# Which routed blocks have their rows turned by the DMA engines: every third instead of every fourth

## The reference

```python
# x: (4096, 512); 16 experts, the top 4 of them for each token
topk_idx, w, _ = _route(xf, router_w, correction_bias)
combine = zeros((S, E)).at[arange(S)[:, None], topk_idx].add(w)
g = einsum('sc,ech->esh', xf, gate_w)      # 512 -> 128 for each expert
u = einsum('sc,ech->esh', xf, up_w)
hw = silu(g) * u * combine.T[:, :, None]
routed = einsum('esh,ehc->sc', hw, down_w) # 128 -> 512
shared_out = silu(xf @ shared_gate_w.T) * (xf @ shared_up_w.T) @ shared_down_w.T
x = x + shared_out + routed
```

## Time and profile before

| what | us |
|---|---|
| three timed runs, median | 1027.05 |
| lowest and highest of them | 1024.96 and 1027.68 |
| the profiled execution, time | 1020.97 |
| the profiled execution, span of the core | 1019.2 |
| PE busy in that span | 995.8 |
| DVE busy | 647.9 |
| POOL busy | 442.3 |
| ACT busy | 381.5 |

### The profile page before, as it was taken

One profiled execution on the slowest core, in us unless ns is written; L12 is line 12 of the kernel. 1 busy time (PEld: TensorE's weight loads), 2 busy tenths in 40 slices (PEclk: granted clock), 3 DMA queues, 4 the chain that ended last, 5 costly groups with the idle time before them and its releaser, 6 DMA issues.

```text
span 1019.2 us, 21258 instructions
## 1 busy us (share of the span) xinstructions
PE 995.8 (98%) x6882; PEld 611.1 (60%) x6882; DVE 647.9 (64%) x1526; ACT 381.5 (37%) x776; POOL 442.3 (43%) x508
## 2 busy tenths in 40 slices
PE   8999998999999999999999999999999999999997
PEld 6685653544544444445778778787777854444443
DVE  5956776566178678977545555555555536687767
ACT  3635534433354334331444444444444431111111
POOL 0814601211134322215444454454454337777774
PEclk9979999999999999999999999999999999999999
DMA  9644786558735351412889989899888758999786
GB/s 339 213 163 135 261 272 187 177 154 262 194 111 168 135 145 63 138 49 72 241 262 252 278 264 272 254 256 260 244 249 255 222 172 233 325 301 319 240 256 206
DMA packets 176636, 219.04 MB, mean 215 GB/s; under 512 B 101224, under 2 KB 112360, under 8 KB 175528
## 3 DMA queue, kind: packets, MB, share of 16 engines
q1 hardware_dynamic: 152792, 139.05, 46.3%
q0 software_dynamic: 23760, 78.79, 25.5%
HBM read 124.72 MB, written 70.27 MB: 191 GB/s over the span
## 4 chain that ended last, share of the span: by engine, by line
PE 76%; POOL 9%; DVE 5%; issue 4%; DMA 3%; ACT 1%; SPq 0%; DVEq 0%; POOLq 0%
PE bank L920 19%; PE bank L1046 18%; POOL arena L2028 9%; PE bank L1070 9%; PE bank L936 9%; PE bank L1029 5%; PE bank L1107 3%; PE bank L693 2%; PE bank L715 2%; PE bank L1060 2%; PE bank L1119 2%; PE bank L782 1%; DMA arena<-in_x 1%; DMA arena<-pt_dram 1%; PE bank L703 1%
## 5 line engine op out<-in xcount | busy, mean ns | idle before, releaser
L920 PE MATMUL bank<-arena 128*128 128x512 f16 x960 | 219.5, 380 | 0.8 <-DMA arena<-pt_dram 0.8
L1046 PE MATMUL bank<-arena 128*128 x1716 | 211.0, 273 | 1.2 <-DVE arena L1587 1.0
L1046 PEld LDWEIGHTS bank<-arena 128*128 128x128 f16 x1716 | 163.1, 98 | 26.8 <-issue 2.0
L1983 POOL DMA_INDIRECT arena<-xr_dram,arena x143 | 140.5, 983 | 59.2 <-issue 48.0
L2028 POOL DMA_INDIRECT arena<-y_dram,arena x128 | 139.7, 1092 | 57.1 <-issue 35.4
L920 PEld LDWEIGHTS bank<-arena 128*128 128x128 f16 x960 | 93.7, 99 | 108.9 <-issue 2.2
L1107 PE MATMUL bank<-arena 128*128 128x512 f16 x576 | 128.1, 379 | 0.0
L1308 ACT ACTIVATE arena<-arena 128x512 f16<-128x512 f32 x64 | 40.3, 629 | 223.4 <-DVE arena L1880 111.9
L1070 PE MATMUL bank<-arena 128*128 x429 | 115.4, 378 | 0.0
L1820 DVE SCALAR_TENSOR_TENSOR arena<-bank,arena 128x128 f32<-128x128 f32 x143 | 41.7, 292 | 108.9 <-ACT arena L1360 108.9
L1872 DVE SCALAR_TENSOR_TENSOR arena<-arena 128x512 f32<-128x512 f32 x128 | 96.1, 752 | 23.1 <-DMA arena<-y_dram,arena 19.6
(11 more groups left out here) (221 smaller groups left out, 1308.0 us busy)
## 6 DMA issues: line engine op xcount, KB each, us to landing
y_dram<-arena SPq DMA_DIRECT2D x143, 256.0 KB
arena<-in_x SPq DMA_DIRECT2D x8, 1024.0 KB, 13.5
xr_dram<-arena SPq DMA_DIRECT2D x16, 512.0 KB, 3.2
x_dram<-arena SPq DMA_DIRECT2D x8, 1024.0 KB, 5.7
arena<-in_gu_w SPq DMA_DIRECT2D x16, 512.0 KB, 3.6
out<-arena SPq DMA_DIRECT2D x32, 256.0 KB, 3.9
arena<-x_dram SPq DMA_DIRECT2D x5, 1024.0 KB, 5.4
arena<-x1s_dram SPq DMA_DIRECT2D x20, 256.0 KB, 4.9
```

What stands on the lines that cost most here:

```text
L920: last = mm(bank[half][:, :], (gu_hi_s, gu_lo_s)[wp][:, c, at:at + H], xt[:, xv * KC + kc, :], start=(n == 0), stop=(n == 3 * KC - 1))
L1046: last = mm(bank[2 + j][:, 0:2 * H], rows[:, xv * KC + kc, :], only((gu_hi_r, gu_lo_r)[wp], e, slice(kc * 2 * H, (kc + 1) * 2 * H)), start ...
L1983: pool.indirect_dma_start(out=dst, out_offset=None, in_=xr_dram[:, :], in_offset=bass.IndirectOffsetOnAxis(ap=token_now[:, r:r + 1], axis= ...
```

## The change

Every third block (s % 3 == 2) is turned by the transposing DMA instead of every fourth (s % 4 == 3): 47 blocks instead of 35, so that PE turns 96 blocks instead of 108. The hardware loops of ACT, DVE and POOL hold 12 blocks instead of 8. The blocks that PE turns have four places for gathered rows instead of three, and the fourth place takes the memory of the fourth `y_sb`, so three result buffers are left. The fourth place may be filled for the first time only after the shared expert's fifth block.

```diff
-UNROLLED = 8
+UNROLLED = 12
...
-        xg = view(o2, [4, 2 * D], F16)
+        xg = [view(v, [2 * D], F16) for v in (o2, o2 + 2 * KB, o2 + 4 * KB, o1 + 2 * KB)]
...
-        y_sb = [view(v, [D]) for v in (o1, o3 + 4 * KB, o3 + 6 * KB, o1 + 2 * KB)]
+        y_sb = [view(v, [D]) for v in (o1, o3 + 4 * KB, o3 + 6 * KB)]
...
         def on_tensor(s):
-            return 3 * (s // 4) + s % 4
+            return 2 * (s // 3) + s % 3
...
                 sp.wait_ge(s_xd[h], 16 * (g // 2 + 1))
                 if g >= 2:
-                    sp.wait_ge(s_rg, 4 * g - 4)
+                    sp.wait_ge(s_rg, 3 * g - 3)
                 sp.dma_start_transpose(xdT[h], xd[h]).then_inc(s_dt[h], 16)
...
             for s in range(BLOCKS):
-                y_out(s, s % 4)
-                if s % 4 == 3 and s + 8 < BLOCKS:
-                    turn_fourth(s // 4 + 2, s // 4 % 2)
+                y_out(s, s % 3)
+                if s % 3 == 2 and s + 6 < BLOCKS:
+                    turn_third(s // 3 + 2, s // 3 % 2)
...
-                if s + 2 < BLOCKS and (s + 2) % 4 != 3:
+                if s + 2 < BLOCKS and (s + 2) % 3 != 2:
                     turn_rows(s + 2)
...
-                    act.wait_ge(s_yw[n % 4], 16 * before)
-                A(y_sb[n % 4], bank[6 + n % 2][:, :], ACT.Copy, scale=1.0 / WS).then_inc(s_ye, 1)
+                    act.wait_ge(s_yw[n % 3], 16 * before)
+                A(y_sb[n % 3], bank[6 + n % 2][:, :], ACT.Copy, scale=1.0 / WS).then_inc(s_ye, 1)
...
-            IN_EIGHT = (3, 0, 1, 2, 7, 4, 5, 6)
-            order = [s for g in range(0, BLOCKS, 4) for s in (g + 3, g, g + 1, g + 2) if s < BLOCKS]
+            IN_TURN = (2, 0, 1, 5, 3, 4, 8, 6, 7, 11, 9, 10)
+            order = [s for g in range(0, BLOCKS, 3) for s in (g + 2, g, g + 1) if s < BLOCKS]
...
-                    if s == 7:
+                    if s == 5:
                         pool.wait_ge(s_sd, FIRST * SH)
-                    if s > 7:
-                        pool.wait_ge(s_dt[s // 4 % 2], 16 * (s // 8))
+                    if s > 5:
+                        pool.wait_ge(s_dt[s // 3 % 2], 16 * (s // 6))
                 else:
-                    dst, done = xg[:, s % 4, :], s_xg[s % 4]
-                    if s >= 4:
-                        pool.wait_ge(s_tx, on_tensor(s) - 2)
+                    p = on_tensor(s)
+                    dst, done = xg[p % 4], s_xg[p % 4]
+                    if p == 3:
+                        pool.wait_ge(s_sd, FIRST * SH)
+                    if p >= 4:
+                        pool.wait_ge(s_tx, p - 3)
```

74 lines of the change are left out of this document (37 added, 37 removed).

## The result

| what | before | after |
|---|---|---|
| median of four runs each, us | 1026.01 | 1053.31 |
| lowest and highest, us | 1016.77 and 1027.68 | 1042.13 and 1073.35 |
| profiled execution, time / span, us | 1020.97 / 1019.2 | 1073.35 / 1071.5 |
| PE busy in the span, us | 995.8 | 1015.1 |

The account below looks back on a forecast made before the run. PE was taken to bound the kernel: 5.4 us less turning, less 1.8 us lost at the start, gives 3.6 us less, 1023.5 us against the median of 1027.05; all other terms nothing. Range 1021.3 to 1029.5 us.

Parts of the forecast that it names:

- What bounds the kernel: Routed stage: PE is busy 50.00 of every 50 us, so each us of work taken from PE is worth a us.
- PE's turning: Routed stage: PE turns 12 blocks fewer at 0.45 us each, 5.4 us less; a group of three takes 7.11 us.
- The start: Start of routed stage: block 3's rows are gathered later, PE waits, and 1.8 us are lost (bounds 0.8 to 2.4).
- The deadline of the transposing DMA: PE needs its result 6.2 us after issue; landing taken as 4.8 to 5.5 us, so no wait.
- POOL's order: The xd gather waits for a landing, three gathers follow in a burst; rows still have 1.7 us and more to spare.
- the second rival: Transposing DMA's deadline missed all the time, possibly feeding itself: 1037 us at 6.5 us landing, 1104 at 8.0; chance 0.18.
- the stretch with nine transposing DMAs: Kernel before, 650 to 700 us: nine transposing DMAs with PE still busy 50.00 us, cited against the second rival.
- Room on the DMA engines: Transposing DMAs rise from 5.2 to 7.0 in 50 us; the rate is no bound, only the latency may be.
- Three result buffers: A y write has 6.5 us to land and took 4.0 us in this stage; cost nothing.
- the free start: Start of routed stage costing nothing; the range's low end, given as 1021.3 us; chance 0.10.
- the third rival: Block 3's rows come as early as PE asks, the start costs nothing, gain up to 5.4 us: 1021.7; chance 0.10.

Follow-up runs that it names:

- e11_both_again: The kernel of e5_both run once more, on a fourth chip: 1059.93 against 1060.74 us for the kernel before, ratio 1.001 (0.9964 to 1.0055).
- e3_no_deadline: Changed kernel, every third block's gate_up reading another block's turned rows without waiting for the transposing DMA, which still runs: 1055.15 us, ratio 1.0331 to the kernel before.
- e1_order: Changed kernel with POOL's gathers in the blocks' own order, the xd gather behind its group's other two: 1041.15 us against 1019.7 for the kernel before.
- e10_third_xd: Changed kernel with a third xd place, three places for PE's rows, POOL's loop over 18 blocks: 1078.33 us against 1057.75 for the kernel before, ratio 1.025.
- e9_more_load: Kernel before plus 12 more same-size transposing DMAs, from DRAM, results unused, its own timing kept: 1027.3 us, ratio 1.0012 (0.9964 to 1.0061).
- e6_late_fourth: Kernel before, its 35 transposing DMAs issued two blocks later, some 6 us ahead of use instead of 11: 1055.36 us, ratio 1.0312.
- e5_both: Changed kernel with gathers in the blocks' own order and each transposing DMA issued two blocks earlier: 1020.0 us, ratio 0.996 to the kernel before.
- e4_parts: Kernel before (35 transposing DMAs) with four gather places, three result buffers, ACT's loop of 12 blocks and POOL's of 16: 1026.39 us, ratio 1.0067.

## Why the prediction was wrong

**What bounds the kernel** was read rightly: PE, and only PE, until the change.

**PE's turning** was right. 768 transposes, and a group of 7.10 us where nothing waits, in e11_both_again (forecast 7.11). The 5.4 us were really taken off PE.

**The start** had its mechanism right and its size wrong. PE's timeline of the changed kernel, and the granted clock from 493.7 to 497 us, in answer to the earlier trace rows:

```profile
493.73 1.03 PE L1029 MATMUL bank<-arena 128*128 128x128 f16 x8 [1.85 <-DMA arena<-xr_dram,arena]
494.56 2.70 PE L1046 MATMUL bank<-arena 128*128 x12
497.10 0.28 PE L1060 MATMUL bank<-arena 128*128 128x128 f16 x2
```

```profile
493.70:497.00 3.30, 3.27 (x20) 2.59 (x21) 0.69 (x1) 0.00 (x0) 2.04 (x5) 0.50 1.02 271
```

The wait of 1.85 us stands where it was forecast, but the clock then fell to 0.50, the lower of its two levels (1.2 GHz), for the next 3.3 us. `turn_h` behind that `gate_up` starts 497.10 - 488.52 = 8.58 us into the stage, against 5.25 us before. 3.3 us are lost instead of 1.8.

**The deadline of the transposing DMA** was mis-sized. The 6.2 us were right, the landing wasn't: 4.8 to 5.5 us were taken, 5.7 us was the median, and the tail reached 10.3 us (the row of line 618 over the routed stage):

```profile
DMA to landing us min/median/max: 3.1/5.7/10.3
```

and that of the gathers, line 1982, in answer to the earlier trace rows:

```profile
DMA to landing us min/median/max: 3.5/5.4/9.6
```

A median below the deadline is not "no wait", since nothing gives back what each late one costs. The evidence for 4.8 us came from a few DMAs under a lighter load; all eight of line 628, from 4.6 to 8.0 us with a median of 7.1 us, some of them in the denser stretch behind the routed stage, were set aside for being elsewhere.

**POOL's order is the step that failed.** It said that with 4.8 us to landing the gathers of the burst would be in time, "1.7 us and more are to spare", and that the burst would lengthen the next transposing DMA by "0.3 to 0.7 us, which the 6.2 us hold". By the same working with the medians measured, 5.7 us for the transposing DMA, 2.0 us to the second gather of the burst and 5.4 us for its landing make 13.1 us against the 12.9 us at which PE wants it: the margin is gone before any of the slow ones. e3_no_deadline shows that this path alone can cost the whole loss. e1_order and e10_third_xd, without it, are still at 1.021 (by the medians) and 1.025, so the mis-sized deadline is not the lesser fault: both failed by the same term, a landing of 4.8 us and little more. The feedback was named in the second rival, "it could feed itself", and then dismissed by the stretch with nine transposing DMAs. That stretch had the load but not the timing: nobody waited for a landing there. e9_more_load and e6_late_fourth say the same with the two swapped: load without the timing 1.0012, timing without the load 1.0312.

**Room on the DMA engines** held as far as the rate goes: e5_both moves up to 272 GB/s at a DMA share of 1.00 to 1.12 with PE busy for 48.42 to 50.00 us of 50 in its six stretches. But it was argued as though rate and latency were apart; the median landing rose from 4.2 us in e4_parts to 6.6 us in e5_both.

**Three result buffers** cost nothing in the changed kernel (0.6 us of ACT's waits), nor in e4_parts, where ACT has no such wait. Where PE keeps its pace under the heavier load they may cost: ACT waits for 16.2 us in e5_both, and some of that reaches PE. In the six stretches of e5_both PE stood idle for 2.7 of 300 us. The 5.4 us less work did not shorten its stage (343.6 against 343.7 us); where the rest of them went, I haven't placed.

**The rivals.** The second happened, but not by its own sum: it priced only the wait ahead of `gate_up`, 0.3 us in each of 45 groups, and that wait was 9.6 us by PE's rows. The larger part stands under the gathers, which came last more often. The Trainium skill ("VectorE: DVE Perf Modes", The three transpose paths), which spoke for it, gives 1309 ns for one square by DMA, by estimate 10.5 us for eight. That is no median of this kernel, but the slowest landing here, 10.3 us, comes near it; no run shows why. In the range, the end for the free start should read 1021.7 us, as in the third rival, and not 1021.3; nothing hangs on it.

What stays open: how much of the loss each of the two ways (rows late, turned block late) carries in a usual run, since they trade places between e1, e3 and e6 and can be late together, as at 544.30; the 0.1 to 1.2% of e4_parts; and what three places do. That the cause is the timing (how late the DMA is issued, and what waits for its landing) and not the number of transposing DMAs is shown by e5_both and e6_late_fourth. That a burst lengthens a landing rests on single cases as those of 525.10, 535.29 and 519.13 and on the medians, not on a run in which the burst alone was changed, and beside each of these DMAs writes of y were on their way too; e5_both and e10_third_xd have long landings with hardly a wait of POOL. So the loop as such is not shown.

## What to carry to other kernels

When a kernel gives one engine's work to a DMA, count the lead time of that DMA in the new rhythm and hold it against the tail of landings under the new load, not against a median under the old. Then ask what the landing releases: an issuing engine that starts to wait for a landing sends its next transfers in bursts, and everything that stands behind the wait in its order is late with it. Whether the bursts also lengthen the next landing, so that the lateness feeds itself, was not shown. Issuing earlier together with taking the other gathers out from behind the wait took back all of the loss here.

## What the runs showed of the hardware that I had not expected

- A stall of PE costs more than its length. After idle times of 1.85 and 3.06 us the granted clock stood at 0.50 from 493.7 to 497 us and at 0.63 from 544.3 to 548.9 us, a `gate_up` took 2.70 and 2.66 us instead of 1.47, and it was back at 0.99 and 1.00 in the stretches after that. After a stall of 1.02 us (524.93) the next `gate_up` took 1.52 us, at a clock of 1.00. Over the 387 us of the routed stage the mean clock was 0.97; 0.03 of 387 is by estimate 11.6 us, the larger part of the 16.8 us (11.4 + 5.4) that PE was busy for beyond its work.
- The same transposing DMA of eight squares landed in 3.1 to 10.3 us, the median moving from 4.2 to 7.0 us between kernels with the same number of them (e4_parts and e6_late_fourth, which differ in the time of issue and in buffers).
- The kernel before took 1019.7, 1024.9, 1057.8 and 1060.7 us in the median on four chips: 4% between chips, more than any of the effects studied.
